# Expert stage of a graph-plus-FFN layer on Trainium2: the buffers of the output rows and the order of gathers and scatters on GpSimd

## Chip, cores and metric

The kernel runs on one core of one Trainium2 chip. The metric is device time in microseconds (us) for one execution, the median over several; lower is better.

## What is computed

The input is `x` (1250 nodes x 1024, fp32), 40000 edges (`src`, `dst`) and weights. Cut to what matters:

```python
x = x + gnn(layernorm(x), src, dst, ...)        # two SAGE layers: h @ W_self + mean_of_neighbours @ W_neigh + b
t = layernorm(x)                                # 1250 x 1024
logits = silu(t @ rw1 + rb1) @ rw2 + rb2        # 8 experts
vals, idx = top_k(logits, 2)
w = softmax(masked logits)                      # two weights per row, zero elsewhere
eh = silu(einsum('td,edh->teh', t, ew1) + eb1)  # hidden size 256
eo = einsum('teh,ehd->ted', eh, ew2) + eb2
out = x + t + einsum('te,ted->td', w, eo)
```

Only the last part, the experts on the rows that chose them, is touched here. Each of the 1250 rows goes to two experts.

## The kernel before, in words

The graph layers, the second layernorm, the router and the sorting of rows by expert come first and are unchanged. They leave, in DRAM, the normalised rows `t_d` and an output `out` that already holds x + t, and in SBUF the tables of the expert stage: which row of `t_d` each slot takes (`ids_i`), which row of `out` it goes to (`to_i`), its weight (`slot_w`) and the expert of each step (`step_x`).

The expert stage has NS = 17 steps. A step serves one expert with one or two blocks of 128 rows; in order of steps 0 to 16 the blocks are 1 2 2 1 2 1 2 2 1 2 2 1 2 1 2 2 1, 27 in all. For each step s:

- SyncE (lines 2018 to 2032) loads the expert's two weight matrices, 1 MB each, into two buffers each.
- GpSimd (lines 2034 to 2066) gathers the step's rows from `t_d`, one indirect DMA for each block (`head`, line 2057), into the step's half of `x_rows`, which has two halves (step s uses half s % 2). `head(s)` first waits, through `m_tx`, until TensorE has transposed the rows of step s - 2. Later it adds the finished rows to `out`, one accumulating indirect DMA for each block (`scatter`, line 2050). `scatter(s)` first waits until the scatters of step s - 1 have landed (lines 2045, 2046), because two scatters may name the same row; then it raises `m_kept` (line 2047) and waits for each block's finished rows (`m_out`, line 2049). The order of the two on GpSimd's queue is written out in lines 2060 to 2066: with LATE = 5, `scatter(s)` stands just before `head(s + 5)`, so `head(s + 4)` is the last gather ahead of it.
- TensorE (lines 2068 to 2123) runs `head(s)`: first product, interleaved with the transposes `turn(s + 1)` (line 2084), and then `tail(s - 1)`: second product of the step before (line 2119). `turn(s + 1)` needs the gather of step s + 1.
- ScalarE (lines 2131 to 2179) takes high parts of weights, rows and hidden, the Silu, and in `shift(s)` (line 2173) fills `o_rows` with slot weight times second bias. It runs `head(s + 1)` before `shift(s)`. `shift(s)` waits for `m_kept` (line 2171).
- VectorE (lines 2181 to 2224) takes low parts and, in `tail(s)` (line 2220), adds slot weight times the second product to `o_rows`.

`o_rows` (line 345) has two halves of two blocks each; step s writes half s % 2, so `shift(s)` has to wait until the scatters of step s - 2 have landed. `m_kept` starts at 1 (the memset of `x_rows`, line 2037) and is raised once by each scatter step after the one before it has landed, so `m_kept >= s + 1` says that. The helper `wait_apart` (lines 363 to 367) is a wait followed by a semaphore increment of its own, which shows in the trace as line 367.

Of the kernel before, what the change touches and what calls it, by code (L numbers as in the profile page):

```python
# [16 lines left out]
F32 = mybir.dt.float32  # L17
# [3 lines left out]
I32 = mybir.dt.int32  # L21
U16 = mybir.dt.uint16
ALU = mybir.AluOpType
ACT = mybir.ActivationFunctionType
AX = mybir.AxisListType
ds = bass.ds

N = 1250
D = 1024
P = 125  # L30
# [27 lines left out]
NX = 8  # L58
# [4 lines left out]
SUB = M // 128  # L63
BIG, SMALL = 10, 7
NS = BIG + SMALL
BLOCKS_IN_USE = BIG * SUB + SMALL
NBLK = BLOCKS_IN_USE + BLOCKS_IN_USE % 2
# [6 lines left out]
assert sorted(ORDER) == list(range(NS))  # L74
BLOCKS = lambda t: SUB if ORDER[t] < BIG else 1
BLOCK_AT = lambda t: min(SUB * ORDER[t], BIG * (SUB - 1) + ORDER[t])
BLOCKS_TO = lambda t: sum(BLOCKS(i) for i in range(t)) if t >= 0 else -SUB
HK = HID // 128
EPS = 1e-5
# [24 lines left out]
def build(nc, I, out):  # L104
    ctx = ExitStack()
    with ctx:
        prog = {k: [] for k in ("sync", "scalar", "vector", "gpsimd", "tensor")}

        def on(engine):

            return prog[engine].append

        def sem(name):
            return ctx.enter_context(nc.semaphore(name))
# [44 lines left out]
        S = Region(R_WORK)  # L159
# [19 lines left out]
        S = Region(R_WORK + RING * G * PW * 2)  # L179
# [6 lines left out]
        S = Region(R_SLAB + 12288)  # L186
        d_rows = S("d_rows", [80, 4, P], I32)
        s_rows = S("s_rows", [80, 4, P], I32)
        S = Region(R_SLAB + 20480)
        d_rowf = S("d_rowf", [80, 4, P], F32)  # L190
        s_rowf = S("s_rowf", [80, 4, P], F32)
        S = Region(R_CONST + 3072)
# [72 lines left out]


        S = Region(R_CONST + 3072)
        rb2b = S("rb2b", [P, NX], F32)
        eb1c = S("eb1c", [128, NX * HK], F32)
        ids_i = S("ids_i", [128, NBLK], I32)  # L270
        to_i = S("to_i", [128, NBLK], I32)
        padi = S("padi", [128, NBLK], I32)
        padf = S("padf", [128, NBLK], F32)
        tok_of = S("tok_of", [128, NBLK], F32)
        slot_w = S("slot_w", [128, NBLK], F32)
        step_x = S("step_x", [1, NS], I32)
        w3 = S("w3", [P, 3, TOP * NT], BF16)
        parts3 = S("parts3", [128, 3 * NBLK], F32)
        S = Region(R_ACC + 33824)
# [43 lines left out]
        S = Region(R_WORK + 8800)  # L323
# [5 lines left out]
        S = Region(R_H)  # L329
# [8 lines left out]
        eb2_all = S("eb2_all", [128, NX, D], F32)  # L338
# [3 lines left out]
        hid = S("hid", [128, 2, HK, M], F32)  # L342
        hid_hi = S("hid_hi", [128, 2, HK, M], F32R)
        assert S.at <= R_WORK + 8800
        o_rows = S("o_rows", [128, 2, SUB, D], F32)
        assert S.at <= R_CONST

        ps = ctx.enter_context(nc.psum_tensor("ps", [128, 8, 512], F32))
# [20 lines left out]
        @on("gpsimd")  # L369
        def _(e):  # L370
            e.memset(zero[:], 0.0).then_inc(s_id, 1)
            e.memset(ident[:], 0.0).then_inc(s_id, 1)
            e.wait_ge(s_id, 2)
            e.affine_select(out=ident[:], in_=ident[:], compare_op=ALU.not_equal, fill=1.0, base=0,
                            pattern=[[-1, 128]], channel_multiplier=1).then_inc(s_id, 1)
            e.memset(ones[:], 1.0).then_inc(s_ones, 1)
            e.memset(epst[:], EPS).then_inc(s_ones, 1)
# [1614 lines left out]
        m_kept = sem("m_kept")  # L1992
# [11 lines left out]
        NB = SUB * 2  # L2004
        GROUP_AT = lambda s: 2 * BLOCKS_TO(s)
        NTH = lambda s, b: 16 * sum(i % 2 == s % 2 and b < BLOCKS(i) for i in range(s + 1))
        WIDE = lambda s: 128 * BLOCKS(s)
        LATE = 5
        w1_view, w2_view = I["L0_ffn_ew1"], I["L0_ffn_ew2"]

        def gated(e):

            e.wait_ge(g_x, 1)
            base_stored(e)
            for u in range(2):
                e.wait_ge(t_st[u], 32 * (NT // 2))
# [17 lines left out]
        @on("gpsimd")  # L2034
        def _(e):
            e.wait_ge(r_log, CHUNKS + 1)
            e.memset(x_rows[:].rearrange("p u b n -> p (u b n)"), 0.0).then_inc(m_kept, 1)
            e.wait_ge(m_kept, 1)
            gated(e)
            e.wait_ge(g_ok, 1)  # L2040
            e.sem_inc(m_tx, 8)

            def scatter(s, u, q):
                if s > 0:
                    for b in range(BLOCKS(s - 1)):
                        e.wait_ge(m_st[1 - u][b], NTH(s - 1, b))
                e.sem_inc(m_kept, 1)
                for b in range(BLOCKS(s)):
                    wait_apart(e, m_out, GROUP_AT(s) + 2 * b + 2 + 2 * NB)
                    e.indirect_dma_start(out=out[:, :], out_offset=bass.IndirectOffsetOnAxis(ap=to_i[:, BLOCK_AT(s) + b:BLOCK_AT(s) + b + 1], axis=0),  # L2050
                                         in_=o_rows[:, u, b, :], in_offset=None,
                                         compute_op=ALU.add).then_inc(m_st[u][b], 16)

            def head(s, u, q):
                wait_apart(e, m_tx, 4 * s + 4)
                for b in range(BLOCKS(s)):
                    e.indirect_dma_start(out=x_rows[:, u, b, :], out_offset=None, in_=t_d[:, :],
                                         in_offset=bass.IndirectOffsetOnAxis(ap=ids_i[:, BLOCK_AT(s) + b:BLOCK_AT(s) + b + 1], axis=0),
                                         bounds_check=N - 1, oob_is_err=False).then_inc(m_xin[u][b], 16)
            for t in range(NS + LATE):  # L2060
                if t == LATE:
                    e.wait_ge(g_to, 1)
                if t >= LATE:
                    scatter(t - LATE, (t - LATE) % 2, (t - LATE) // 2)
                if t < NS:
                    head(t, t % 2, t // 2)
# [64 lines left out]
        @on("scalar")  # L2131
        def _(e):
            gated(e)
            e.wait_ge(g_eb, 32)

            def w1(s, u, q):
                e.wait_ge(m_win[0][u], 16 * q + 16)
                e.wait_ge(m_g1, HK * s + HK)
                e.activation(w1_hi[:, u], w1_raw[:, u], ACT.Copy).then_inc(m_whi[0], 1)

            def w2(s, u, q):
                e.wait_ge(m_win[1][u], 16 * q + 16)
                e.wait_ge(m_g2, GROUP_AT(s - 1) + 2 * NB)
                e.activation(w2_hi[:, u], w2_raw[:, u], ACT.Copy).then_inc(m_whi[1], 1)  # L2144

            def rows(s, u, q, groups=range(4)):
                for g in groups:
                    e.wait_ge(m_tx, 4 * s + g + 1 + 8)
                    e.activation(group(xt_hi, s, u, g), bank(s, g), ACT.Copy).then_inc(m_xhi, 1)

            def head(s, u, q):
                x = e.value_load(step_x[0:1, ds(ORDER[s], 1)], min_val=0, max_val=NX - 1)
                if more(s):
                    w1(s + 1, 1 - u, q + u)
                for j in range(HK):
                    wait_apart(e, m_g1, HK * s + j + 1 + 4)
                    e.activation(hid[:, u, j, 0:WIDE(s)], ps[:, 2 + j, 0:WIDE(s)], ACT.Silu, bias=eb1c[:, ds(x * HK + j, 1)]).then_inc(m_h, 1)
                    if more(s):
                        rows(s + 1, 1 - u, q + u, range(2 * j, 2 * j + 2))
                    if j == 0:  # L2160
                        w2(s, u, q)
                e.wait_ge(m_h, HK * s + HK + 2)
                e.wait_ge(m_g2, GROUP_AT(s - 1) + 2 * NB)
                e.activation(hid_hi[:, u, :, 0:WIDE(s)], hid[:, u, :, 0:WIDE(s)], ACT.Copy).then_inc(m_hhi, 1)

            def shift(s, u, q):
                x = e.value_load(step_x[0:1, ds(ORDER[s], 1)], min_val=0, max_val=NX - 1)
                if s == 0:
                    e.wait_ge(g_to, 2)
                    e.wait_ge(g_b2, 16)  # L2170
                e.wait_ge(m_kept, s + 1)
                for b in range(BLOCKS(s)):
                    e.activation(o_rows[:, u, b, :], eb2_all[:, ds(x, 1), :].rearrange("p a n -> p (a n)"), ACT.Copy,
                                 scale=slot_w[:, BLOCK_AT(s) + b:BLOCK_AT(s) + b + 1]).then_inc(m_eb, 1)

            e.sem_inc(m_out, 2 * NB)
            w1(0, 0, 0)
            rows(0, 0, 0)
            pipeline(e, NS, (0, head), (1, shift))

        @on("vector")
        def _(e):
# [31 lines left out]
            def tail(s, u, q):  # L2214
                for b in range(BLOCKS(s)):
                    e.wait_ge(m_eb, BLOCKS_TO(s) + b + 1)
                    for half in range(2):
                        e.wait_ge(m_g2, GROUP_AT(s) + 2 * b + half + 1 + 2 * NB)
                        cols = o_rows[:, u, b, 512 * half:512 * half + 512]
                        e.scalar_tensor_tensor(out=cols, in0=ps[:, 4 + 2 * b + half, :], scalar=slot_w[:, BLOCK_AT(s) + b:BLOCK_AT(s) + b + 1],  # L2220
                                               in1=cols, op0=ALU.mult, op1=ALU.add).then_inc(m_out, 1)
            w(0, w1_raw, w1_hi, w1_lo, 0, 0, 0)
# [44 lines left out]
```

## Time and profile before

| | |
|---|---|
| runs, median (lowest to highest) | 1129.91 us (1129.89 to 1142.7), 3 runs |
| profiled execution, its own time | 1135.2 us |
| its span, first to last instruction | 1133.0 us |
| busy share of the span: TensorE, weight load, VectorE, ScalarE, GpSimd | 94%, 89%, 54%, 38%, 16% |
| mean granted TensorE clock | 0.968 of full speed |
| HBM read, written | 108.40 MB, 42.96 MB |

How to read what follows: PE is TensorE, PEld its weight load, DVE VectorE, ACT ScalarE, POOL GpSimd, SP SyncE; a name with q is that engine's sequencer (waits, semaphores). Queue q0 carries the indirect DMAs that GpSimd issues, q1 the loads that SyncE issues. "DMA share" is the mean busy share of the 16 DMA engines. In a timeline each row is start, duration, engine, line, operation, output<-input, count, and in brackets the idle time before it with what ended it. Times run from the start of the span; the expert stage fills about 890 to 1133 us.

### The profile page before, as it was taken

What the parts mean: (1) busy time and instruction counts of PE and PEld (TensorE: products, weight loads), DVE (VectorE), ACT (ScalarE), POOL (GpSimd) and SP (SyncE); (2) the same over time, 40 slices, a digit from 0 to 9 for tenths busy, and PEclk for the clock granted to TensorE, in tenths of its full rate; (3) what the DMA queues carried; (4) which work ended last, traced back from release to release, by engine and by line L of the source; (5) the groups of instructions that cost most, each with busy time, mean ns of one, the idle gap of its engine ahead of it and who ended that gap; (6) DMA issues with size and microseconds to landing.
All of it is one profiled execution on the core that took longest, in us unless ns stands there. A gap on an engine that the chain in (4) does not pass through costs nothing.

```text
span 1133.0 us, 17970 instructions
## 1 busy us (share of the span) xinstructions
PE 1060.1 (94%) x6444; PEld 1011.8 (89%) x6444; DVE 616.1 (54%) x1093; ACT 428.2 (38%) x934; POOL 185.3 (16%) x194
## 2 busy tenths in 40 slices
PE   4999999999989999999998999999999299999992
PEld 3999999999989999999998999999999199999892
DVE  6678888888652343235222523363221767888672
ACT  5555444453311312121122012263322366767661
POOL 5500000000000011001100110004450215444332
PEclk9999999999989999999999999999999569999996
DMA  7332133212217650033103320385554269999965
GB/s 192 88 101 71 46 102 106 92 49 73 97 42 237 189 153 1 1 99 103 29 1 106 96 51 1 98 261 156 164 156 168 99 255 324 301 350 298 294 118 90
DMA packets 72793, 148.86 MB, mean 131 GB/s; under 512 B 11867, under 2 KB 50712, under 8 KB 68210
## 3 DMA queue, kind: packets, MB, share of 16 engines
q1 hardware_dynamic: 61041, 112.50, 30.9%
q0 software_dynamic: 10976, 34.65, 12.5%
q8 instruction: 67, 1.10, 0.4%
q10 hardware_dynamic: 672, 0.32, 0.1%
q14 instruction: 37, 0.30, 0.1%
HBM read 108.40 MB, written 42.96 MB: 134 GB/s over the span
## 4 chain that ended last, share of the span: by engine, by line
PE 73%; DMA 12%; issue 5%; DVE 5%; PEld 2%; POOL 1%; DVEq 1%; ACT 1%; POOLq 0%; ACTq 0%; PEldq 0%
PE ps L1464 20%; PE ps L941 14%; DMA out<-o_rows,to_i 11%; PE ps L1536 10%; PE ps L1503 9%; PE ps L1195 8%; PE ps L813 4%; PE ps L2098 2%; PEld ps L737 2%; POOL out L2050 1%; PE ps L2119 1%; PE ps L909 1%; PE ps L2084 1%; DVE key_hot L806 1%; PE ps L1522 1%
## 5 line engine op out<-in xcount | busy, mean ns | idle before, releaser
L1426 POOL TENSOR_TENSOR s_rows<-s_rows,b1t 125x1368 f32<-125x1368 f32 (+3 forms) x9 | 23.5, 2630 | 583.3 <-DMA s_rows<-in_x 583.3
L820 DVE TENSOR_TENSOR adj<-ps,adj 125x250 f32 x212 | 87.9, 415 | 41.8 <-PE ps L813 33.6
L941 PE MATMUL ps<-h_lo,w_hi 128*128 128x418 f32 x336 | 108.6, 372 | 0.0
L941 PE MATMUL ps<-h_hi,w_hi 128*128 128x418 f32 x336 | 100.2, 379 | 0.0
L1503 PE MATMUL ps<-z_lo,adj 125*125 125x342 f32 (+1 forms) x300 | 95.4, 323 | 2.7 <-issue 2.7
L1503 PE MATMUL ps<-z_hi,adj 125*125 125x342 f32 (+1 forms) x300 | 96.0, 325 | 2.0 <-DVE s_rows L1735 2.0
L941 PE MATMUL ps<-h_hi,w_lo 128*128 128x418 f32 x336 | 93.5, 359 | 0.0
L2187 DVE TENSOR_TENSOR w_lo<-w_raw,w_hi 128x2048 fp32r<-128x2048 f32 x34 | 77.9, 2290 | 28.3 <-ACT w_hi L2144 21.4
L1195 PE MATMUL ps<-adj,y_hi 125*128 125x416 f32 (+1 forms) x240 | 86.4, 360 | 3.4 <-issue 3.4
L1195 PE MATMUL ps<-adj,y_lo 125*128 125x416 f32 (+1 forms) x240 | 86.1, 359 | 0.7 <-issue 0.7
L813 PE MATMUL ps<-key_hot,src_hot 125*125 125x250 bf16 x424 | 80.8, 271 | 3.3 <-DVE adj L820 3.1
L2098 PE MATMUL ps<-xt_hi,w_hi 128*128 128x256 f32 (+1 forms) x272 | 79.8, 293 | 1.0 <-issue 1.0
L2098 PE MATMUL ps<-xt_lo,w_hi 128*128 128x256 f32 (+1 forms) x272 | 78.8, 290 | 0.0
L2098 PE MATMUL ps<-xt_hi,w_lo 128*128 128x256 f32 (+1 forms) x272 | 78.7, 290 | 0.0
L1464 PE MATMUL ps<-wn_hi,hs_lo 128*125 128x342 f32 (+1 forms) x240 | 76.7, 320 | 0.0
L1464 PE MATMUL ps<-wn_hi,hs_hi 128*125 128x342 f32 (+1 forms) x240 | 76.7, 320 | 0.0
L1464 PE MATMUL ps<-ws_hi,hs_hi 128*125 128x342 f32 (+1 forms) x240 | 76.7, 320 | 0.0
L1464 PE MATMUL ps<-ws_lo,hs_hi 128*125 128x342 f32 (+1 forms) x240 | 76.7, 319 | 0.0
L1464 PE MATMUL ps<-ws_hi,hs_lo 128*125 128x342 f32 (+1 forms) x240 | 76.6, 319 | 0.0
L1464 PE MATMUL ps<-wn_lo,hs_hi 128*125 128x342 f32 (+1 forms) x240 | 76.5, 319 | 0.0
L813 PEld LDWEIGHTS ps<-key_hot,src_hot 125*125 125x125 bf16 x424 | 56.6, 136 | 18.7 <-issue 6.9
L806 DVE TENSOR_TENSOR key_hot<-seq,key_now 125x1000 bf16<-125x1000 f16 x106 | 71.3, 672 | 0.0
(304 smaller groups left out, 2655.8 us busy)
## 6 DMA issues: line engine op xcount, KB each, us to landing
w_raw<-in_L_ffn_ew SPq DMA_DIRECT2D x34, 1024.0 KB, 8.5
xin<-in_x SPq DMA_DIRECT2D x10, 448.0 KB
t_d<-xn SPq DMA_DIRECT2D x10, 448.0 KB
base<-x_d POOLq DMA_DIRECT2D x10, 448.0 KB, 4.2
out<-base POOLq DMA_DIRECT2D x10, 448.0 KB, 3.5
y_d<-y_hi SPq DMA_DIRECT2D x7, 625.0 KB
y_d<-y_lo SPq DMA_DIRECT2D x7, 625.0 KB
self_d<-self SPq DMA_DIRECT2D x7, 625.0 KB
```

The source lines that it names most:

```text
L737: mm = e.matmul(FIRST_BANK(own, c), wt[:, own, k, :], ht[:, k, a:a + w], start=(n == 0), stop=(n == 3 * KT - 1))
L806: ins = e.tensor_tensor(both(hot).rearrange("p c (v x) -> p c v x", x=2), seq, place, ALU.is_equal)
L813: mm = e.matmul(ps[0:P, 5 + b % 2, 0:KW], src_hot[:, b, g, 0:P], key_hot[:, b, g, :], start=(g == 0), stop=(g == G - 1))
L820: e.tensor_tensor(cols, ps[0:P, 5 + b % 2, 0:KW].rearrange("p (t w) -> p t w", t=NT), cols, ALU.add).then_inc(self.took, 1)
L941: mm = e.matmul(BANK(m, own, c), wt[:, own, k, :], ht[:, k, a:a + w], start=(k == 0 and p == 0), stop=(k == KT - 1 and p == 2))
L1195: mm = e.matmul(ps[:, banks[c], 0:w], y[:, k, :], adj_[:, k, a:a + w], start=(n == 1), stop=(n == 2 * NT))
L1426: e.tensor_tensor(cols, cols, b1t[:, 0:w].rearrange("p (a n) -> p a n", a=1).to_broadcast([P, n, w]), ALU.add).then_inc(s_x, 1)
L1464: mm = e.matmul(ps[0:P, 2 * v + u, 0:w], ht[:, u, k, :], wt[v][:, k, 0:w], start=(k == EARLY[0] and p == 0), stop=(k == LATE_K[-1] and p = ...
L1503: mm = e.matmul(ps[0:P, 2 + n % 2, 0:w], adj_[:, k, tile_of(j)], z[:, k, 0:w], start=(k == 0 and p == 0), stop=(k == NT - 1 and p == 1))
L1536: mm = e.matmul(ps[:, i % 5, 0:w], wt[u][:, k, :], ht[:, k, a:a + w], start=(n == 1), stop=(n == 3 * KT))
L2098: mm = e.matmul(ps[:, 2 + j, 0:WIDE(s)], wt[:, u, k, 128 * j:128 * j + 128], xt[:, u, k, 0:WIDE(s)], start=(n == 1), stop=(n == 3 * KT))
L2187: e.tensor_tensor(lo[:, u], raw[:, u], hi[:, u].bitcast(F32), ALU.subtract).then_inc(m_wlo[i], 1)
```

## The change

- `o_rows` becomes a list of five blocks of 128 x 1024; block number n of the whole stage (0 to 26) uses block n % 5. Four lie where the two halves lay, the fifth (`o_fifth`) over tables that are no longer read by then; five small tables change places for it.
- `shift(s)` waits for each block on its own: where block n - 5 belongs to step r, it waits for `m_kept >= r + 3`, which says that the scatters of step r have landed. The first five blocks don't wait. In this program r is s - 3 for the last block of every step from the fourth on.
- LATE goes from 5 to 6: `scatter(s)` now stands just before `head(s + 6)` on GpSimd's queue, so `head(s + 5)` stands ahead of it.

```diff
+O_RING = 5
+STEP_OF = [t for t in range(NS) for _ in range(BLOCKS(t))]
...
         S = Region(R_CONST + 3072)
-        rb2b = S("rb2b", [P, NX], F32)
         eb1c = S("eb1c", [128, NX * HK], F32)
         ids_i = S("ids_i", [128, NBLK], I32)
         to_i = S("to_i", [128, NBLK], I32)
+        slot_w = S("slot_w", [128, NBLK], F32)
+        step_x = S("step_x", [1, NS], I32)
+        o_fifth = Region(S.at)("o_fifth", [128, D], F32)
+        rb2b = S("rb2b", [P, NX], F32)
         padi = S("padi", [128, NBLK], I32)
         padf = S("padf", [128, NBLK], F32)
         tok_of = S("tok_of", [128, NBLK], F32)
-        slot_w = S("slot_w", [128, NBLK], F32)
-        step_x = S("step_x", [1, NS], I32)
...
-        o_rows = S("o_rows", [128, 2, SUB, D], F32)
+        o_rows = [S(f"o_rows{i}", [128, D], F32) for i in range(4)] + [o_fifth]
...
-        LATE = 5
+        o_row = lambda s, b: o_rows[(BLOCKS_TO(s) + b) % O_RING]
+        LATE = 6
...
-                                         in_=o_rows[:, u, b, :], in_offset=None,
+                                         in_=o_row(s, b)[:], in_offset=None,
...
-                e.wait_ge(m_kept, s + 1)
                 for b in range(BLOCKS(s)):
-                    e.activation(o_rows[:, u, b, :], eb2_all[:, ds(x, 1), :].rearrange("p a n -> p (a n)"), ACT.Copy,
+                    older = BLOCKS_TO(s) + b - O_RING
+                    if older >= 0:
+                        e.wait_ge(m_kept, STEP_OF[older] + 3)
+                    e.activation(o_row(s, b)[:], eb2_all[:, ds(x, 1), :].rearrange("p a n -> p (a n)"), ACT.Copy,
                                  scale=slot_w[:, BLOCK_AT(s) + b:BLOCK_AT(s) + b + 1]).then_inc(m_eb, 1)
...
-                        cols = o_rows[:, u, b, 512 * half:512 * half + 512]
+                        cols = o_row(s, b)[:, 512 * half:512 * half + 512]
```

## Rows read from the trace of the kernel before

**Rows 1.** Chain that ended last, 935 to 1133 us, shares by line.
```profile
by line: DMA out<-o_rows,to_i 64.1%; issue 12.4%; POOL out L2050 6.4%; PE ps L2119 4.9%; PE ps L2098 4.8%; PE ps L2084 1.3%; POOLq L2233 0.9%; DVE o_rows L2220 0.4%; POOLq L367 0.2%; POOLq L2047 0.1%; POOLq L2057 0.0%; DVEq L2218 0.0%
```

**Rows 2.** Waits, 935 to 1133: who waited for whom, us, times, longest.
```profile
POOL out L2050 <- DMA out<-o_rows,to_i: 71.7, 12, 9.2
...
POOL x_rows L2057 <- PE ps L2084: 18.1, 8, 3.5
...
ACT o_rows L2173 <- POOLq L2047: 9.6, 2, 6.0
```

**Rows 3.** Timeline of GpSimd, first gathers and scatters, 935 to 972.
```profile
935.84 2.83 POOL L2050 DMA_INDIRECT out<-o_rows,to_i  x1 [1.33 <-DVE o_rows L2220]
940.94 1.66 POOL L2057 DMA_INDIRECT x_rows<-t_d,ids_i  x1 [2.27 <-PE ps L2084]
945.96 1.59 POOL L2050 DMA_INDIRECT out<-o_rows,to_i  x1 [3.35 <-DVE o_rows L2220]
...
953.49 1.32 POOL L2057 DMA_INDIRECT x_rows<-t_d,ids_i  x1 [3.52 <-PE ps L2084]
955.11 1.19 POOL L2057 DMA_INDIRECT x_rows<-t_d,ids_i  x1 [0.30 <-DMA out<-o_rows,to_i]
957.77 1.62 POOL L2050 DMA_INDIRECT out<-o_rows,to_i  x1 [1.47 <-DVE o_rows L2220]
...
965.59 1.65 POOL L2057 DMA_INDIRECT x_rows<-t_d,ids_i  x1 [3.09 <-PE ps L2084]
967.54 1.02 POOL L2057 DMA_INDIRECT x_rows<-t_d,ids_i  x1 [0.30 <-issue]
971.11 1.62 POOL L2050 DMA_INDIRECT out<-o_rows,to_i  x1 [2.54 <-DMA out<-o_rows,to_i]
```

**Rows 4.** Timeline of GpSimd, last gathers and scatters, 1043 to 1125.
```profile
1043.72 3.33 POOL L2050 DMA_INDIRECT out<-o_rows,to_i  x1 [0.30 <-issue]
...
1058.28 1.61 POOL L2050 DMA_INDIRECT out<-o_rows,to_i  x1 [8.52 <-issue]
...
1062.07 1.75 POOL L2057 DMA_INDIRECT x_rows<-t_d,ids_i  x1 [0.30 <-issue]
...
1074.01 1.62 POOL L2050 DMA_INDIRECT out<-o_rows,to_i  x1 [8.85 <-DMA out<-o_rows,to_i]
1075.93 1.03 POOL L2057 DMA_INDIRECT x_rows<-t_d,ids_i  x1 [0.31 <-issue]
1080.98 1.59 POOL L2050 DMA_INDIRECT out<-o_rows,to_i  x1 [4.02 <-DMA out<-o_rows,to_i]
...
1094.74 1.56 POOL L2050 DMA_INDIRECT out<-o_rows,to_i  x1 [9.16 <-DMA out<-o_rows,to_i]
1101.98 1.56 POOL L2050 DMA_INDIRECT out<-o_rows,to_i  x1 [5.67 <-DMA out<-o_rows,to_i]
...
1112.85 1.56 POOL L2050 DMA_INDIRECT out<-o_rows,to_i  x1 [5.48 <-DMA out<-o_rows,to_i]
...
1122.78 1.56 POOL L2050 DMA_INDIRECT out<-o_rows,to_i  x1 [6.50 <-DMA out<-o_rows,to_i]
```

**Rows 5.** Line 2050, scatters issued in 935 to 1080: landing times.
```profile
DMA to landing us min/median/max: 6.0/9.4/13.6
```

**Rows 6.** Windows: busy PE, PEld, DVE, ACT, POOL; clock, DMA share, GB/s.
```profile
935.00:1080.00 145.00, 142.13 (x991) 132.13 (x991) 115.08 (x126) 101.69 (x132) 61.41 (x38) 0.99 1.00 310
1080.00:1115.00 35.00, 32.19 (x206) 28.88 (x204) 22.39 (x27) 19.47 (x24) 12.80 (x7) 0.99 0.58 107
```

**Rows 7.** Timeline of TensorE around its one stall after 935.
```profile
1077.42 1.94 PE L2084 MATMUL ps<-ident,x_rows 128*128 128x128 f32 x8 [2.87 <-issue]
```

**Rows 8.** Line 2050, scatters issued in 1095 to 1133: landing times.
```profile
DMA to landing us min/median/max: 6.0/6.3/8.1
```

**Rows 9.** Line 2031, the weight loads that SyncE issues: first and last start.
```profile
L2031 SPq DMA_DIRECT2D w_raw<-in_L_ffn_ew x34: 332/337/650, 892.8 to 1084.2; - x34
```

**Rows 10.** DMA queue of GpSimd, 935 to 1133: packets, MB, share of 16 engines.
```profile
q0 software_dynamic: 6912, 22.30, 52.1%
```

## Prediction, written before the changed kernel was run

> **What bounds the kernel now.** I read the chain that ended last first, over the expert stage. From 935 us on it is not TensorE: 64.1% of the stretch is scatters in flight, 12.4% the short steps between them and 6.4% their issue, against some 11% for TensorE's three lines together [rows 1]. The waits say how: before a scatter GpSimd waited 12 times for an earlier scatter's landing, 71.7 us in all [rows 2]. So the end is a chain of scatters, each issued about 0.9 us after the one before has landed.
>
> The timeline of GpSimd shows where that chain begins. The scatters of steps 0 to 2 start at 935.84, 945.96 and 957.77 and are released by VectorE, that is by the products; the one of step 3 at 971.11 is released by a landing [rows 3], and so are the later ones to the last at 1122.78 [rows 4] (step 10's row at 1058.28 says "issue", but the block before it went out at 1043.72, and with the longest landing, 13.6 us [rows 5], it was there at 1057.3, 1.0 us before). From 957.77 to 1122.78 these are 14 steps in 165.0 us, 11.8 each. TensorE meanwhile does its steps in less: it is busy for 142.13 of 145 us up to 1080, with one stall [rows 6, 7], and for 32.19 us from then, so it is done at about 1112 [rows 6], and the last scatter, one block, still goes out at 1122.78. So 10 us of lag are built up on the way.
>
> Why the links are long shows in the windows and landings: from 935 to 1080 the 16 DMA engines are busy all the time (share 1.00), from 1080 on 0.58 [rows 6]. A scatter takes 9.4 us to land in the first stretch (median) and 6.3 us at the end [rows 5, 8].
>
> **The change, part by part.**
>
> *The ring.* It takes away what made ScalarE wait for a scatter two steps back. That cost ScalarE 9.6 us in two waits, the longest 6.0 us [rows 2]. Neither lies on the chain of scatters: from 971.11 on each scatter goes out after a landing, not after VectorE [rows 3, 4]. The number of operations stays: 27 fills on ScalarE, 54 additions on VectorE, 27 gathers, 27 scatters. There are 22 waits in place of 17, and what a wait costs that is already met I bound by nothing and by the 0.3 us that stand between two issues on GpSimd [rows 3], so 0 to 1.5 us on ScalarE, which is idle for 43 of 145 us [rows 6]. I take 0. Behind a waiting fill on ScalarE stand the next high parts, the Silu and so TensorE; with the ring the wait is for the step three back.
>
> *The order on GpSimd.* The gather of step s + 5 now stands ahead of scatter s, with its wait. That wait is for the transposes of step s + 3, which TensorE does inside the first product of step s + 2, one step later than the second product of step s that the scatter needs. So the scatter, ready as before, is held for about a TensorE step until that gather is out. The rows give the size. Scatter 0 went at 935.84; the gather of step 5 went at 940.94, released by the transposes, and took 1.66 us, so scatter 0 can go at about 942.9: 7.1 us later. Scatter 1 went at 945.96; the two gathers of step 6 end at 955.11 + 1.19 = 956.3, so it goes at 956.6: 10.6 later. Scatter 2 went at 957.77; the gathers of step 7 end at 967.54 + 1.02 = 968.6, so 968.9: 11.1 later [rows 3]. From there on the chain of landings decides again, as 1 to 2 took 11.8 us before and 956.6 + 11.8 = 968.4 is all but the same. With links as they were, every scatter to the last comes 11.1 us later. For steps 0 to 2 this is a wait by TensorE's pace, which nothing hides since the chain has no slack behind it.
>
> *What it brings forward.* The gathers of steps 5 to 13 gain nothing: they went out just after the transposes that free their half of `x_rows` (8 waits, 18.1 us [rows 2]), and those don't move. The last three were held by scatters in front of them. That of step 15, at 1062.07 behind scatter 10 [rows 4], is the one that TensorE then lacked: it stood still for 2.87 us before the transposes at 1077.42 [rows 7]. Now it stands behind scatter 9, whose second block ends at 1043.72 + 3.33, with the late start 1058.2: 3.9 us earlier, so this stall goes and TensorE gains 2.9 us. That shortens no chain by itself, because TensorE is done 10 us before the last scatter; but weights and gathers end earlier, at about 1077 in place of 1080, and the DMA engines are free for scatters from then.
>
> *What comes back.* On the old time scale 1077 less 11.1 is 1066, in the link from scatter 10 (1058.28) to 11 (1074.01), 15.7 us long, with 8 us to go [rows 4]. A link of two blocks without load is 1101.98 to 1112.85 and 1112.85 to 1122.78, on average 10.4 us [rows 4]. The 8 us become 8 x 10.4 / 15.7 = 5.3, so 2.7 us come back. The link 11 to 12 took 7.0 us, as short as an unloaded one (1094.74 to 1101.98, 7.2), and returns nothing. The link 12 to 13 took 13.8 us, with the last weights, issued at 1084.2 [rows 9], in flight; those now land before it, so 10.4 us, and 3.4 come back. Together 6.1; the last weights take something of it where they now fall, on link 10 or 11, and I take 6. Its bounds are 0, if every link is as long as it was, and 20, if the whole late start is caught up in the loaded stretch and all links from scatter 10 on are unloaded: 10.4 + 7 + 10.4 + 7.2 + 10.4 + 10.4 = 55.8 in place of 64.5 from 1058.28 to 1122.78. Between these I lean to the low half because the nearest rows show the chain already without a pause under load: eight links from 957.77 to 1058.28, 12.6 us each [rows 3, 4].
>
> *Sum.* +11.1 - 6 = +5 us. On the profiled execution's own time, 1135.2 (span 1133.0 and 2.2 around it), this is 1140. The median of the runs is 5.3 below that execution, so the forecast for the median is 1129.9 + 5 = 1135 us. The term's bounds are +11.1 and 11.1 - 20 = -9, so 1141 and 1121.
>
> **Rivals.**
>
> *A: nothing comes back, +11, 1141 us.* The start is late by a step, the links are as before, and the earlier end of weights and gathers only meets other scatters. For it: a link depends on what is in flight beside it, and each scatter now meets the gather of one step later at about the same point of its flight. Against it: at the end there is nothing left to meet.
>
> *B: not slower, because the DMA engines are the bound, -3, 1127 us.* The stretch to 1080 has share 1.00 [rows 6]. q0's 52.1% of 198 us over the 46 gathers and scatters issued in it are 2.2 us of all engines for each [rows 10], so the scatters of one step, 1.6 blocks, that are not in flight are 3.5 us of engine time for the others. If the engines do the same work without a gap, gathers and weights of the early steps land sooner, and the scatters have the engines more to themselves later: the ten links from 2 to 12, 123.2 us or 12.3 each, would be 1.1 us shorter each, giving the 11.1 back, and the link 12 to 13 is 3.4 shorter. It decides if those ten links come out at 11.2 us or less on average. Against it: an early saving is of use only if something is waiting, and the next gather and weights wait for TensorE and VectorE, not for DMA, so the engines would stand still in the first 25 us. The Trainium skill, "DMA: Bandwidth & Descriptors", section "Issuing engines are not separate DMA queues", states that DMAs from all issuing engines run on the same 16 engines and interleave; by that rule moving a scatter would move work, not add it, which is this rival. The rows that agree are the share of 1.00 and the landings of 9.4 against 6.3 us.
>
> *C: the lag starves ScalarE, +25, 1155 us.* From the step where scatters are more than three steps behind, `shift` holds VectorE's additions behind it and then TensorE. A stall like the one at 1077 costs 2.9 us [rows 7]; nine would make 25. Against it: the scatter that is waited for is one step older and comes one step later, so ScalarE's slack is as before, when it waited twice in 17 steps [rows 2].
>
> *D: the links collapse, -25, 1105 us*, which would need the chain to end before TensorE does, and TensorE itself to be shorter.
>
> **How the numbers follow.** The forecast, +2 to +8, has 0.46; A 0.25; B, from -7 to +1, 0.23; C 0.04; D 0.02. The range for 8 in 10 reaches over most of A and B: 1124 to 1144. For the three classes, 2% of the time is 22.6 us, about what a measurement of this kernel can tell from no change. Forecast, A and B lie within it, 0.94; C is slower, 0.04; D faster, 0.02.
>
> **What would show it.** Right: in the timeline of GpSimd the first three scatters start near 943, 957 and 969, each just after a gather and not just after VectorE; the gathers of step 15 go out near 1058; TensorE has no stall near 1075; the last scatter goes out near 1128, after a landing; scatters still take most of the chain. Wrong: the first scatters start where they did (then the order holds nothing back); or the links from 2 to 12 average 11.2 us or less (B); or the last scatter is 11 us later (A); or ScalarE waits long at its fills and TensorE stalls in the middle (C).

## The result, and the profile after

The changed kernel takes 1145.3 us (median of 20 runs, 1137.5 to 1150.5) against 1129.9 for the kernel before on the same chips (20 runs, 1117.8 to 1147.3). The ratio is 1.0169, 95% interval 1.0144 to 1.0193, so some 16 to 22 us slower. Executions of one kernel fall into a faster and a slower group: the medians here and below are over all executions, the ratios compare the faster group alone and need not equal the quotient of two medians. The direction was forecast, the size was not: 1135 was forecast, with 1124 to 1144 as the range. The profiled execution took 1149.6 us, its span is 1147.4 us, 14.4 more than before; in this execution the expert stage starts 1.8 us earlier than in the one of before (first gather at 896.57 and 898.35), so the stage itself is 16.2 us longer. Each kernel has one trace, and these two are of executions 5.3 and 4.3 us above their medians. All lags below are counted from that first gather.

The chain that ended last, over the expert stage of the changed kernel, shares by line (the fifth block appears under its own name; the view of [rows 1]):

```profile
by line: DMA out<-o_rows,to_i 62.4%; issue 11.5%; POOL out L2054 6.2%; DMA out<-o_fifth,to_i 6.1%; PE ps L2102 3.8%; PE ps L2123 2.6%; PE ps L2088 1.1%; POOLq L2239 0.8%; POOL x_rows L2061 0.7%; POOLq L370 0.2%; POOLq L2051 0.2%; POOLq L206
```

It is the same chain: 68.5% scatters in flight where it was 64.1%. The timeline of GpSimd from the gather of step 5 on (the view of [rows 3]; line 2054 is the scatter, 2061 the gather):

```profile
939.08 1.63 POOL L2061 DMA_INDIRECT x_rows<-t_d,ids_i  x1 [6.42 <-PE ps L2088]
941.01 1.64 POOL L2054 DMA_INDIRECT out<-o_rows,to_i  x1 [0.30 <-issue]
951.64 1.32 POOL L2061 DMA_INDIRECT x_rows<-t_d,ids_i  x1 [8.99 <-PE ps L2088]
953.27 1.17 POOL L2061 DMA_INDIRECT x_rows<-t_d,ids_i  x1 [0.30 <-issue]
954.75 1.61 POOL L2054 DMA_INDIRECT out<-o_rows,to_i  x1 [0.30 <-issue]
...
968.75 2.10 POOL L2054 DMA_INDIRECT out<-o_rows,to_i  x1 [1.99 <-issue]
...
984.93 3.38 POOL L2054 DMA_INDIRECT out<-o_rows,to_i  x1 [10.03 <-DMA out<-o_fifth,to_i]
...
998.32 1.61 POOL L2054 DMA_INDIRECT out<-o_rows,to_i  x1 [5.25 <-DMA out<-o_rows,to_i]
...
1002.11 2.36 POOL L2061 DMA_INDIRECT x_rows<-t_d,ids_i  x1 [0.30 <-issue]
...
1061.87 1.60 POOL L2054 DMA_INDIRECT out<-o_fifth,to_i  x1 [6.73 <-DMA out<-o_rows,to_i]
...
1137.16 1.55 POOL L2054 DMA_INDIRECT out<-o_rows,to_i  x1 [6.65 <-DMA out<-o_rows,to_i]
```

Scatters 0 and 1 go out 0.3 us after a gather that waited for TensorE's transposes: the wait by VectorE is gone from their rows and another, later one stands in its place. Their lag is 7.0 and 10.6 us. From scatter 2 on it is landings again that release them (for scatter 2 the row says "issue", but scatter 1's second block, out at 956.67, landed after 11.2 us, 0.9 us before it). But the lag doesn't stay: scatter 9 (1061.87, before 1041.82) is 21.8 us late, and scatter 16 (1137.16, before 1122.78) is 16.2 us late. A link is the time from one step's first scatter to the next step's. So the time divides into three: +10.6 up to scatter 1, +11.3 over the eight links from 1 to 9 (13.4 us each in place of 12.0), and -5.7 over the seven links from 9 to 16 (10.8 in place of 11.6).

The landing times of scatters, line 2054, first those issued in 935 to 1080 and then those in 1095 to 1148 (the views of [rows 5, 8]):

```profile
DMA to landing us min/median/max: 6.1/10.7/13.2
...
DMA to landing us min/median/max: 6.0/6.7/7.8
```

At the end they are nearly as before (6.3); in the loaded stretch, while weights are still being loaded, the median is 10.7 in place of 9.4. The DMA engines are not busier for it. The windows (the view of [rows 6]) have a DMA share of 0.92 up to 1080, where it was 1.00:

```profile
935.00:1080.00 145.00, 140.07 (x938) 129.65 (x937) 109.86 (x123) 98.80 (x128) 61.25 (x37) 0.95 0.92 286
1080.00:1115.00 35.00, 35.00 (x238) 32.17 (x237) 24.73 (x28) 20.56 (x27) 9.20 (x4) 1.00 0.63 148
```

TensorE has its stall too, only earlier and longer than the one of [rows 7]:

```profile
1043.17 1.94 PE L2088 MATMUL ps<-ident,x_rows 128*128 128x128 f32 x8 [4.75 <-issue]
```

The transposes are of a step of two blocks, step 12. The row names no releaser. Step 12's first gather, issued at 1026.33, landed after 13.0 us; for its second, issued at 1028.61, the views give no landing, but the last event of its semaphore in the trace is at 1043.08, 0.1 us before the transposes. So it is the gather which is late, as before at 1077. And the waits (the view of [rows 2]) show that the ring did not end ScalarE's:

```profile
POOL out L2054 <- DMA out<-o_rows,to_i: 81.2, 12, 9.0
...
POOL x_rows L2061 <- PE ps L2088: 23.8, 6, 9.0
...
POOL out L2054 <- DMA out<-o_fifth,to_i: 10.0, 1, 10.0
...
ACT o_rows L2179 <- POOLq L2051: 7.7, 2, 4.8
...
ACT o_fifth L2179 <- POOLq L2051: 4.1, 1, 4.1
```

11.8 us where it was 9.6: with scatters later by more than a step, three steps back is as late as two steps back was.

### The profile page after: what moved, and what is told of

The parts are those of the page before. It is cut to its first block, busy times and chain, and to the rows that moved or that the text cites. A ratio compares the mean times of both kernels' runs of the same rounds, so it can differ in the third digit from the quotient of the medians.

```text
span 1147.4 us, 17970 instructions
## 1 busy us (share of the span) xinstructions
PE 1062.6 (93%) x6444; PEld 1013.6 (88%) x6444; DVE 615.9 (54%) x1093; ACT 427.6 (37%) x934; POOL 186.6 (16%) x194
## 4 chain that ended last, share of the span: by engine, by line
PE 72%; DMA 13%; issue 5%; DVE 4%; PEld 2%; POOL 2%; ACT 1%; DVEq 1%; POOLq 0%; ACTq 0%; PEldq 0%
PE ps L1467 20%; PE ps L944 14%; DMA out<-o_rows,to_i 12%; PE ps L1539 10%; PE ps L1198 8%; PE ps L1506 8%; PE ps L816 4%; PE ps L2102 2%; PEld ps L740 1%; POOL out L2054 1%; DMA out<-o_fifth,to_i 1%; PE ps L912 1%; PE ps L2088 1%; DVE key_hot L809 1%; PE ps L1525 1%
```

## The experiments

Two theories stood at first. Theory 1: the late start of the first scatters is all, carried to the end. Theory 2: the new order lengthens the links in the loaded stretch besides. The rival to both was the ring. Times are medians in us, with the median of the kernel before on the same chip; the ratio has its 95% interval.

**e1, the order alone,** in the kernel before.

```diff
-        LATE = 5
+        LATE = 6
```

> The kernel before with LATE = 6 alone, two step buffers kept. Theory 1 (the order holds the first scatters back by a TensorE step and nothing gives it back): as slow as the changed kernel, 13 to 20 us above before; first scatters 7 and 10.6 us late by the timeline. Rival (the ring costs it, by its per-block waits or the place of the fifth block): within 4 us of before.

1154.1 against 1127.1, ratio 1.0236 (1.0156 to 1.0316): 27 us slower, more than the whole change and than the 13 to 20 expected. The waits tell why it is more:

```profile
ACT o_rows L2173 <- POOLq L2047: 47.5, 12, 9.6
```

With two halves ScalarE waits 12 times for a late scatter, and TensorE behind it is done 19 us later than before (232.7 us after the first gather in place of 213.8). So the order is the cost, and the ring takes a part of it away.

**e2, the ring alone:** the changed kernel with the old order.

```diff
-        LATE = 6
+        LATE = 5
```

> The changed kernel with LATE = 5: the ring alone. Theory 1: within 4 us of before, on the faster side if on any, first scatters where they were. Rival (the ring costs it): 10 to 16 us above before.

1133.7 against 1127.1, ratio 1.0052 (1.0008 to 1.0096). Not the cause of 1.7%. It is not on the faster side either, though ScalarE's waits are gone and TensorE has no stall (busy 145.00 of 145 us up to 1080, done 4.6 us earlier): that time is not on the chain, whose scatters go out about 0.9 us after a landing from scatter 3 to the last. (The chain view of this trace names TensorE's lines up to scatter 13, for 74.4%; but scatter 13, out at 1090.73, follows the landing of scatter 12, 1079.44 + 10.4, by 0.9 us too. Landing and products came together there, so TensorE's work is a second limit close behind.) Why it is half a per cent slower stays open; in its profiled execution the stage is 2 us shorter.

**e3, the first three scatters as early as before.** In the changed kernel scatters 0 to 2 stand behind the gathers up to step s + 4, those from 3 on behind s + 5.

```diff
-            for t in range(NS + LATE):
-                if t == LATE:
-                    e.wait_ge(g_to, 1)
-                if t >= LATE:
-                    scatter(t - LATE, (t - LATE) % 2, (t - LATE) // 2)
-                if t < NS:
-                    head(t, t % 2, t // 2)
+            gathered = 0
+            for s in range(NS):
+                while gathered < min(NS, s + (5 if s < 3 else LATE)):
+                    head(gathered, gathered % 2, gathered // 2)
+                    gathered += 1
+                if s == 0:
+                    e.wait_ge(g_to, 1)
+                scatter(s, s % 2, s // 2)
```

> The changed kernel, but scatters 0 to 2 stand behind one gather less, as before; from scatter 3 on the order is the changed one. Theory 1: the late start is gone and with it nearly all, within 5 us of before. Theory 2 (the late start is only part; a gather issued right ahead of a scatter on the same queue makes each link under load longer): 6 to 12 us above before, links of steps 3 to 8 on average over 13 us in place of 12.

1144.3 against 1127.1, ratio 1.0167 (1.0081 to 1.0253): as slow as the changed kernel. Theory 1, within 5 us, falls; theory 2 had said 6 to 12. GpSimd's timeline shows the lag come back within three steps:

```profile
956.56 1.62 POOL L2054 DMA_INDIRECT out<-o_rows,to_i  x1 [1.37 <-DVE o_fifth L2227]
...
974.24 1.30 POOL L2061 DMA_INDIRECT x_rows<-t_d,ids_i  x1 [6.79 <-PE ps L2089]
975.84 1.86 POOL L2054 DMA_INDIRECT out<-o_rows,to_i  x1 [0.30 <-issue]
987.20 1.22 POOL L2061 DMA_INDIRECT x_rows<-t_d,ids_i  x1 [9.50 <-PE ps L2089]
988.72 1.47 POOL L2061 DMA_INDIRECT x_rows<-t_d,ids_i  x1 [0.30 <-issue]
990.49 1.62 POOL L2054 DMA_INDIRECT out<-o_rows,to_i  x1 [0.30 <-issue]
992.41 1.86 POOL L2054 DMA_INDIRECT out<-o_rows,to_i  x1 [0.31 <-issue]
...
1007.52 3.53 POOL L2054 DMA_INDIRECT out<-o_rows,to_i  x1 [7.91 <-DMA out<-o_rows,to_i]
```

Scatter 2 is on time. Scatters 3 and 4 stand 0.3 us behind a gather that had to wait for TensorE, and the one after needs 17.0 us, with a landing of 14.2. By scatter 8 this kernel is as late as the changed one (152.8 and 153.5 us after the first gather). From scatter 9 on, though, this execution gives back some 13 us where the changed one gives back 5.7, and its last scatter is 7.8 us late. Its time, 1142.4, is the lowest of its four, and the execution of before beside it lies 5.3 us above its median: this pair shows less of the cost than the medians do. The lateness is not handed on from the start; the order makes it wherever a scatter would be early.

**e4, one gather more ahead** in the changed kernel.

```diff
-        LATE = 6
+        LATE = 7
```

> The changed kernel with LATE = 7: the suspected cost doubled. Theory 1: first scatters another 10 to 11 us later, 24 to 32 us above before in all. Theory 2: the start as in theory 1, and the links about as long as with LATE = 6, so the same within 4 us of that. Rival (the scatters' start doesn't reach the end of the kernel): about 15 us above before, as with LATE = 6.

1159.0 against 1127.1, ratio 1.0270 (1.0188 to 1.0351): some 30 us slower. The first scatter goes at 956.59, 58.2 us after the first gather in place of 44.4 and 37.5. Both theories had this range; what it excludes is the rival that the scatters' start doesn't reach the end.

After these the question was what lengthens the links. Two candidates: the weight loads that a scatter now meets (2a), or the gathers ahead of it on its own queue (2b). Each was halved in both kernels, so that the two can be compared with the same bytes.

**e5 and e6, half weights, in the changed kernel and in the one before.** From step 2 on only the first half of each matrix is loaded; the products use what an earlier step left in the other half.

```diff
-                    e.dma_start(raw[:, u], view[ds(x, 1)].rearrange("a p k n -> p (a k) n")).then_inc(m_win[w][u], 16)
+                    k = (KT, HK)[w] // (1 if s < 2 else 2)
+                    e.dma_start(raw[:, u, 0:k], view[ds(x, 1), :, 0:k].rearrange("a p k n -> p (a k) n")).then_inc(m_win[w][u], 16)
```

> The changed kernel; from step 2 on each weight load fetches only the first half of its matrix (1 MB less for each step; the products use stale halves). Theory 2a (each scatter now goes out together with a burst of weights and gathers and shares the DMA engines with it, so its landing is longer): links of steps 3 to 9 fall from 13 to 11 us or less, and the kernel comes within 6 us of the kernel before with the same half loads. Theory 2b (the gathers ahead of the scatters on the same queue lengthen the landing): links stay at 12.5 to 13, and 12 to 20 us remain between the two. Rival (the wait ahead of the gather holds each scatter): 12 to 20 us remain too, with scatters released by gathers and not by landings.

> The kernel before with the same half weight loads, the yardstick for the run above. All theories: faster than before, as TensorE ends at about 1107 to 1112 us and the scatters can follow it closely: 5 to 14 us less than before.

1129.3 (changed) and 1124.3 (before); the kernel before with full weights had 1133.6 on this chip, ratios 1.0023 (0.9987 to 1.0060) and 0.9966 (0.9930 to 1.0002). Of the 15 to 19 us between the two, 4.9 are left. The links from 1 to 9 are 11.5 us in both. The kernel before gains 0 to 8 us by its ratio, mostly under the 5 to 14 expected. The waits of GpSimd, first of the changed kernel and then of the one before with half weights:

```profile
POOL x_rows L2062 <- PE ps L2089: 52.9, 12, 9.0
...
POOL out L2055 <- DMA out<-o_rows,to_i: 38.1, 8, 6.5
```

```profile
POOL out L2051 <- DVE o_rows L2221: 42.8, 14, 8.1
...
POOL x_rows L2058 <- PE ps L2085: 36.9, 12, 4.0
...
POOL out L2051 <- DMA out<-o_rows,to_i: 8.3, 2, 6.1
```

With the order of before, scatters now wait for VectorE, that is for the products, and twice for a landing. With the changed order it is the gathers that wait, 16 us longer, with the scatters behind them: the scatters keep TensorE's pace, a step late. That is the late start of the prediction, and with half the weights, where links no longer depend on the order, it is worth what the forecast said, 5 us.

**e7 and e8, half gathers, in the changed kernel and in the one before.** Each gather fetches rows 0 to 63 of its block; the others keep what was there.

```diff
-                    e.indirect_dma_start(out=x_rows[:, u, b, :], out_offset=None, in_=t_d[:, :],
-                                         in_offset=bass.IndirectOffsetOnAxis(ap=ids_i[:, BLOCK_AT(s) + b:BLOCK_AT(s) + b + 1], axis=0),
+                    e.indirect_dma_start(out=x_rows[0:64, u, b, :], out_offset=None, in_=t_d[:, :],
+                                         in_offset=bass.IndirectOffsetOnAxis(ap=ids_i[0:64, BLOCK_AT(s) + b:BLOCK_AT(s) + b + 1], axis=0),
```

> The changed kernel; each gather fetches 64 of its 128 rows (0.25 MB less for each block; the other rows are stale). Theory 2b: landings of scatters fall by 2 us and more, and the kernel comes within 6 us of the kernel before with the same half gathers. Theory 2a: landings fall by 1 us or less, 10 to 18 us remain between the two.

> The kernel before with the same half gathers, the yardstick for the run above. All theories: 2 to 10 us less than before, since fewer bytes share the DMA engines.

1148.5 and 1137.4 against 1133.6: ratios 1.0186 (1.0110 to 1.0261) and 1.0039 (0.9992 to 1.0086). 11.1 us are left between the two, and neither got faster. The landing of scatters issued in 935 to 1080, changed and before with half gathers:

```profile
DMA to landing us min/median/max: 6.3/10.4/13.1
```

```profile
DMA to landing us min/median/max: 7.2/11.2/13.4
```

In the changed kernel it is 0.3 us less than with full gathers, as 2a had it; 2b falls. That the kernel before gained nothing and its landings grew from 9.4 to 11.2 was expected by no theory, and the cause stays open.

**e9, e10 and e11, the two weight loads apart.** The rows of SyncE show a pattern that had been overlooked: the second weights of one step and the first of the next go out within about 2 us of each other, then nothing for 8 to 12 us (up to 16 in the changed kernel). Timelines around scatter 4, of the changed kernel (SyncE's pair of loads, then the scatters of two blocks) and of the kernel before:

```profile
996.71 1.43 SPq L2035 DMA_DIRECT2D w_raw<-in_L_ffn_ew  x2
...
998.32 1.61 POOL L2054 DMA_INDIRECT out<-o_rows,to_i  x1 [5.25 <-DMA out<-o_rows,to_i]
...
1000.23 1.57 POOL L2054 DMA_INDIRECT out<-o_rows,to_i  x1 [0.31 <-issue]
```

```profile
975.82 1.42 SPq L2031 DMA_DIRECT2D w_raw<-in_L_ffn_ew  x2
...
982.88 1.59 POOL L2050 DMA_INDIRECT out<-o_rows,to_i  x1 [6.18 <-DMA out<-o_rows,to_i]
...
984.78 1.58 POOL L2050 DMA_INDIRECT out<-o_rows,to_i  x1 [0.31 <-issue]
```

Their landings, changed and before, each of the two blocks alone:

```profile
DMA to landing us min/median/max: 10.5/10.8/11.1
```

```profile
DMA to landing us min/median/max: 6.5/6.9/7.3
```

The same scatter lands in 10.5 and 11.1 us when it goes out 1.6 us after the pair begins, and in 6.5 and 7.3 when it goes out 7 us after. Counted in this way for scatters 3 to 8, the last load lay 3.7, 6.0, 2.5, 6.2, 5.4 and 4.9 us back before the change, and 9.8, 0.5, 2.2, 0.6, 3.1 and 0.2 after it (the first of these goes out 2 us ahead of the next pair; each number is the scatter's start less that of the last load).

The six traces with full weights in pairs (before, changed and e1 to e4) show the same together. These are the first blocks of the steps, issued before 1080, by the time since the last load went out:

| since the last load | scatters | landing, median (lowest to highest) |
|---|---|---|
| less than 2 us | 21 | 10.7 us (8.4 to 13.4) |
| 2 to 4 us | 22 | 9.9 us (6.9 to 12.0) |
| 4 to 6 us | 9 | 7.4 us (6.0 to 10.5) |
| more than 6 us | 10 | 6.5 us (6.1 to 7.7) |

Five more, over 5 us after a load but within 2.5 us ahead of the next, take 9.2 to 13.7. Among scatters 1 to 8, none goes out within 2 us of a load with the old order (before, e2), and three or four do with the later ones (changed, e1, e3, e4).

To test the timing without a change in bytes, the loads were put apart:

```diff
-            def head(s, u, q):
-                x = e.value_load(step_x[0:1, ds(ORDER[s], 1)], min_val=0, max_val=NX - 1)
-                for w, (raw, view) in enumerate(((w1_raw, w1_view), (w2_raw, w2_view))):
...
-            pipeline(e, NS, (0, head))
+            def load(w, raw, view):
+                def one(s, u, q):
+                    x = e.value_load(step_x[0:1, ds(ORDER[s], 1)], min_val=0, max_val=NX - 1)
...
+                return one
+            pipeline(e, NS, (0, load(0, w1_raw, w1_view)), (1, load(1, w2_raw, w2_view)))
```

> The changed kernel; SyncE issues the first weights of step s + 1 ahead of the second weights of step s, so that the two loads of 1 MB go out some 5 us apart and not within 2 us of each other. All bytes are as before. Theory 2a in its narrow form (it is the burst of two loads at one time that a scatter meets): links of steps 2 to 9 fall from 13.3 to 12 us, and the kernel comes within 9 us of the kernel before with the same loads. Theory 2c (only the sum of bytes counts, not their time): links stay above 13 us and 12 to 20 us remain between the two.

> The kernel before with the two weight loads apart. Narrow 2a: links of 12 us become 11 to 11.5, and the end 3 to 10 us earlier. 2c: within 3 us of before.

> The ring with LATE = 5 and the two weight loads apart. Within 4 us of the kernel before with the loads apart by either theory; by narrow 2a faster than before by 3 to 10 us.

Changed 1141.5, before 1139.3, ring alone 1142.4, against 1131.1: ratios 1.0134 (1.0068 to 1.0201), 1.0103 (1.0050 to 1.0155) and 1.0116 (1.0062 to 1.0171). The difference between the two orders shrank to 2.2 us, as theory 2a said, but from the other side: the changed kernel hardly moved (links from 1 to 9 of 12.7 us), and the kernel before lost its lead: its links from 1 to 9 became 13.0 us where they were 12.0, with the same bytes in the same order on GpSimd's queue. Its landings in 935 to 1080, of which the view holds only the second blocks of seven steps with two:

```profile
DMA to landing us min/median/max: 10.4/11.3/14.4
```

The same seven blocks of the kernel before took 7.3 to 13.6, median 9.5. Of the eight links from 1 to 9 those behind such steps are the longer ones. Behind steps of one block they are shorter or the same, as from 5 to 6, 8.4 us in place of 12.9:

```profile
1003.11 1.61 POOL L2051 DMA_INDIRECT out<-o_rows,to_i  x1 [10.48 <-DMA out<-o_rows,to_i]
...
1011.54 1.62 POOL L2051 DMA_INDIRECT out<-o_rows,to_i  x1 [4.17 <-DMA out<-o_rows,to_i]
```

e10 and e11 were expected to be faster and are slower, so the narrow form of 2a, that the burst is the harm, falls. So does 2c, that only the sum of the bytes counts and not their time: it wanted 12 to 20 us between e9 and e10, and e10 within 3 us of before. What is left is that a pair of loads at one time leaves a gap behind it, and that the kernel before puts more of its scatters into the gap. This last step is read from the traces above. No version tried here that loads all the weights beats the kernel before.

## Why the prediction was right or wrong, point by point

- *What bounds the kernel*: right. The chain of scatters ends last in both kernels, and e2 shows that time saved on ScalarE and TensorE is not on it. But the chain begins earlier than was read: before the change scatters 1 and 2, which the rows put down to VectorE [rows 3], also go out 0.9 us after a landing, of scatter 0 (935.84 + 9.2) and of scatter 1's second block (947.86 + 9.0). The products were ready at about the same moment, and a row names one releaser only.
- *The order on GpSimd, the late start*: right to half a microsecond for scatters 0 and 1 (7.1 and 10.6 forecast, 7.0 and 10.6 measured), 12.8 in place of 11.1 for scatter 2. Scatter 2 was no longer held by a gather: it went out 0.9 us after scatter 1's second block (956.67 + 11.2) had landed, which had taken 9.0 us before, so the first longer link is already in its lag.
- *"With links as they were, every scatter to the last comes 11.1 us later"*: this step failed. The links were taken as fixed, but a link depends on when its scatter goes out beside the weight loads. The links from 1 to 9 grew from 12.0 to 13.4 us, 11.3 us in all: that is the missing term, and with it the sum is 10.6 + 11.3 - 5.7 = 16.2 us, what the profiled execution shows. Rival A had the assumption in its own words, that each scatter meets the gather at about the same point; the row that would have warned is the spread of landings, 6.0 to 13.6 [rows 5], which the prediction used only as a median. e3 shows that the order makes the term and not the late start, e5 and e6 that it belongs to the weights (4.9 us are left without half of them), and e10 that their timing counts. That the changed kernel's scatters meet the loads more often is read from the traces; no run moved all its scatters back into the gap with the order kept.
- *What comes back*: 6 forecast, 5.7 measured, and the agreement is luck. Of the links that were named, 12 to 13 gave back 3.6 us (3.4 forecast), but 10 to 11 gave nothing (2.7 forecast) and 11 to 12 became 3.2 longer. What came back lies in the link from 9 to 10, 16.5 us before and 10.6 after, which the forecast did not name.
- *What it brings forward*: wrong. The gathers of steps 5 to 13 were said not to move. They do once the chain is more than a step late, because each now stands behind a scatter that waits for a late landing: step 10's went out at 1002.11, 6 us later than before counted from the first gather (it was at 997.74), and step 15's, forecast for 1058, at 1066.33. The stall that was to go moved to 1043 and grew from 2.87 to 4.75 us.
- *The ring*: right that it is worth nothing by itself (e2: half a per cent slower), and too short: with the changed order it carries some 8 us, the difference of e1's 27 and the change's 19 by their ratios (e1's interval is wide, 18 to 36, but each of its four times is above all of the changed kernel), since the two halves would have stalled ScalarE for 47.5 us.
- *Rivals*: A came nearest to the median, by its end and not by its reason. B was refuted: it needed links of 11.2 us or less from 2 to 12, they came out at 13.0, and the DMA share fell from 1.00 to 0.92. The rule of the Trainium skill that stood with it ("DMA: Bandwidth & Descriptors", section "Issuing engines are not separate DMA queues": all DMAs run on the same 16 engines and interleave) agrees with e5 and e6, where fewer bytes of weights shorten the scatters' landings up to 1080 (median 8.9 in place of 10.7, and 7.7 in place of 9.4); but it does not make the moment indifferent, as the landings by time since the last load show. C's stalls came in e1 and e4 only (TensorE busy for 130.0 and 130.1 of the 145 us up to 1080).

## What to carry to other kernels

On a queue that works in order, putting a DMA ahead of another puts its wait ahead too: ask not only whether the moved one is wanted earlier but what its wait does to the chain behind it. In a loop whose transfers are issued at a fixed point of each step, a transfer on the critical chain has good and bad moments; take its duration from rows at the moment at which it would go out after the change, not from a median. An experiment that removes the late start alone (e3) was worth more than the sum of the terms: it showed that the order, not the start, sets the lag.

## What the runs showed of the hardware that was not expected

In these two kernels the landing of a 0.5 MB accumulating scatter lies between 6 and 14 us by what else is in flight, and by when: 6.0 to 6.3 us at the end of the kernel before with no load in flight (the first blocks of scatters 13 to 16), 6.5 to 7.3 some 7 us after a pair of 1 MB loads, 10.5 to 11.1 when issued 1.6 us after it. Spreading the same loads over the step made the links of the kernel before 13.0 us in place of 12.0, and the kernel 1.0% slower. Halving the bytes of the gathers on GpSimd's own queue changed the landings of the changed kernel by 0.3 us; those of the kernel before grew by 1.8, for a reason that is not known.
